# A graph attention product cut from 128 moving columns to the 32 of its head

## The reference

```python
h = (x @ W).reshape(n, heads, head_dim)            # 2048 x 4 x 32
src = jnp.einsum('nhd,d->nh', h, a[:head_dim, 0])
dst = jnp.einsum('nhd,d->nh', h, a[head_dim:, 0])
e = src[:, :, None] + dst.T[None, :, :]
e = jnp.where(e > 0, e, ALPHA * e)
e = jnp.where(mask, e, NEG_INF)
attn = jax.nn.softmax(e, axis=-1)
out = jnp.einsum('nhm,mhd->nhd', attn, h)           # the graph product
```

## Time and profile before

| what | value |
|---|---|
| median of 3 runs | 3480.16 us (3479.34 to 3480.24) |
| the profiled execution | 3477.87 us |
| its span, first to last instruction | 3476.2 us |
| PE busy | 2180.2 us (63%), 13842 records |
| PEld busy | 1526.6 us (44%) |
| DVE busy | 1950.8 us (56%) |
| ACT busy | 1052.5 us (30%) |
| POOL busy | 2078.4 us (60%) |
| mean granted TensorE clock | 0.774 of 2.4 GHz |

### The profile page before, as it was taken

The page is one execution under the profiler, slowest core; times in us unless marked ns, Lnnn a source line. Parts: engine busy times, 40 slices in busy tenths (PEclk is TensorE's granted clock), DMA queues, the critical chain, the costliest instruction groups (busy, mean ns, idle before and its releaser), DMA issues.

```text
span 3476.2 us, 42178 instructions
## 1 busy us (share of the span) xinstructions
PE 2180.2 (63%) x13842; PEld 1526.6 (44%) x13842; DVE 1950.8 (56%) x6499; ACT 1052.5 (30%) x1958; POOL 2078.4 (60%) x2078
## 2 busy tenths in 40 slices
PE   4425445555656565666666676868685767674776
PEld 4323333334334343444444454645463444454555
DVE  3577756565565656565757574747574521216543
ACT  2222222232222322333333333424242323232332
POOL 0026557777777777767777776767676777750000
PEclk7666666676777777777878787979797879887888
DMA  1013233434343334343434343333333344432110
GB/s 55 14 38 90 85 96 106 125 107 124 109 121 106 122 108 121 108 123 106 128 103 131 99 123 106 112 115 106 107 104 110 112 122 120 119 93 92 67 55 19
DMA packets 164634, 348.20 MB, mean 100 GB/s; under 512 B 38816, under 2 KB 91712, under 8 KB 160192
## 3 DMA queue, kind: packets, MB, share of 16 engines
q0 software_dynamic: 98624, 269.62, 26.4%
q1 hardware_dynamic: 65792, 75.90, 6.7%
HBM read 333.83 MB, written 11.53 MB: 99 GB/s over the span
## 4 chain that ended last, share of the span: by engine, by line
POOL 38%; PE 23%; issue 15%; DVE 14%; ACT 6%; DVEq 2%; DMA 2%; SPq 0%; ACTq 0%; POOLq 0%
POOL ring L571 38%; PE acc L652 9%; PE turn L643 5%; DMA ring<-in_kv_table,idxT 2%; PE wide L662 2%; PE rowsum L624 1%; DVE kv L1035 1%; ACT att_p L875 1%; PE turn L334 1%; PE wide L325 1%; DVE kv L1024 1%; ACT pt_sb L806 1%; DVE pos L1091 1%; DVE sims L1083 1%; ACT att_p L886 1%
## 5 line engine op out<-in xcount | busy, mean ns | idle before, releaser
L571 POOL DMA_INDIRECT ring<-in_kv_table,idxT x2048 | 2067.8, 1010 | 1028.7 <-issue 614.2
L624 PE MATMUL rowsum<-ring,w_block 128*32 128x256 f32 x4096 | 371.4, 464 | 512.7 <-DMA ring<-in_kv_table,idxT 487.7
L652 PE MATMUL acc<-kv,pt_sb 128*128 128x128 f32 x3968 | 623.5, 313 | 84.6 <-ACT pt_sb L806 84.5
L652 PEld LDWEIGHTS acc<-kv,pt_sb 128*128 128x128 f32 x3968 | 566.6, 222 | 130.8 <-ACT pt_sb L806 130.8
L806 ACT ACTIVATE pt_sb<-turn 128x512 f32<-128x512 f32 (+2 forms) x608 | 331.6, 562 | 474.1 <-PE turn L643 472.8
L624 PEld LDWEIGHTS rowsum<-ring,w_block 128*32 128x32 f32 x4096 | 103.6, 121 | 742.3 <-DMA ring<-in_kv_table,idxT 560.6
L643 PE MATMUL turn<-ident,kv 128*128 128x128 f32 x1280 | 253.1, 349 | 183.7 <-ACT kv L877 101.8
L643 PEld LDWEIGHTS turn<-ident,kv 128*128 128x128 f32 x1280 | 203.7, 184 | 233.5 <-issue 179.6
L730 PE MATMUL wide<-kv,qT 128*128 128x512 f32 (+3 forms) x576 | 261.0, 587 | 29.1 <-ACT att_p L886 20.7
L1048 DVE TENSOR_REDUCE att_m<-wide 128x1 f32<-128x128 f32 (+14 forms) x120 | 146.6, 1222 | 145.1 <-PE wide L730 140.4
L290 POOL DMA_DIRECT2D out<-ring x4 | 3.1, 773 | 362.5 <-DVE ring L453 362.5
(11 more groups left out here) (220 smaller groups left out, 3189.9 us busy)
## 6 DMA issues: line engine op xcount, KB each, us to landing
kv<-in_adj SPq DMA_DIRECT2D x32, 1024.0 KB, 5.0
ring<-in_kv_table,idxT POOLq DMA_INDIRECT x2048
wq_pair<-in_Wq SPq DMA_DIRECT2D x64, 128.0 KB
v_dram<-sums_sb SPq DMA_DIRECT2D x128, 64.0 KB
kv<-v_dram SPq DMA_DIRECT2D x16, 512.0 KB
att_p<-in_Wo SPq DMA_DIRECT2D x16, 512.0 KB, 4.7
xt<-in_x SPq DMA_DIRECT2D x16, 64.0 KB, 3.9
x_dram<-x SPq DMA_DIRECT2D x16, 64.0 KB, 2.2
```

Source lines behind the costliest of these rows:

```text
L571: pool.indirect_dma_start(ring[:, slot, i, :], None, kv_table, bass.IndirectOffsetOnAxis(idxT[:, r % 3, u:u + 1], 0))\
L624: mm = pe.matmul(rowsum[32 * k:32 * k + 32, 0:ROW], w_block[:, at:at + 32], ring[:, slot, k, :], start=(tk == 0), stop=(tk == 3))
L652: mm = pe.matmul(dst, pt_sb[:, q % 2, b * P:(b + 1) * P], rhs(4 * q + b), start=(q + b == 0), stop=(q == len(widths) - 1 and b == widths[q ...
```

## The change

In the call of `turn_and_sum` for the graph product, the moving operand becomes the 32 columns of head s instead of all 128 columns of h, and the result goes to the 32 columns of `acc` that line 1043 reads. Stationary operand, number of instructions, waits and buffers stay.

```diff
@@ -749,7 +749,8 @@
                     pe.wait_ge(gat_exp, m + 1)
                     after(pe, gat_out, m)
                     turn_and_sum(masked_dst, [4] * CH, gat_turned, gat_copied, m * CH,
-                                 lambda b: h_all[:, b * P:(b + 1) * P], acc[:, 2 * P:3 * P]).then_inc(gat_summed, 1)
+                                 lambda b: h_all[:, b * P + s * GD:b * P + (s + 1) * GD],
+                                 acc[:, 2 * P + s * GD:2 * P + (s + 1) * GD]).then_inc(gat_summed, 1)
                 if main:
                     pe.wait_ge(p_made, met(q, 2 * s) + 1)
                     scores_of(2 * s + 1)
```

## The result

The changed kernel takes 3587.24 us (median of 4 runs, 3584.24 to 3589.10) against 3480.20 us before (4 runs). The ratio is 1.0307, with a 95% interval of 1.0289 to 1.0325: 107 us slower. The number of instructions is the same, 42178.

What follows compares the result with a forecast made beforehand. No engine bounds the whole; POOL sets the pace from some 500 us to 3100 us. 78.4 + 2.6 + 10 - 1.4 = 89.6 us more on 3477.9 gave a forecast of 3568 us, range 3474 to 3600.

Steps and rivals of the forecast that it cites:

- part 1: Graph products on PE: a record costs the same at 8, 32 and 128 columns, so 0.00 us change for each.
- The small term of part 1: End of each graph product: the last record leaves the array sooner, 0.05 us each, 28 x 0.05 = 1.4 us gained.
- part 2: Graph products on PE: the clock doesn't rise within a changed product, 2.8 us lost for each, 28 x 2.8 = 78.4 us.
- (a): Graph products: clock rises as before and pace is as before, about 3479 us; chance 0.20.
- (b): Graph products: the clock rises in some products or later in them, 3490 to 3525 us; chance 0.10.
- First rounds: First four rounds: all 16 graph products on the path lose 2.8 us each, and line 704 loses 2.6 us in all.
- Step 3 of the later rounds: Rounds n = 1 to 12: the 12 graph products of step 3 have no cover and lose 2.8 us each.
- Rival (c): Graph products: narrow records run quicker than their weight loads suggest, 0.067 us each, 50 us gained, 3428 us; chance 0.12.
- the one for the late rounds: Last four graph rounds: PE's cover shrinks, 2.5 us lost on each, 10 us in all, bounds 0 and 34.

Runs made afterwards that it cites:

- the third experiment: Only the 12 graph products of step 3 in rounds n = 1 to 12 take 32 columns, against the kernel before: 3510.24 us, ratio 1.0085.
- The kernel with fillers: Changed kernel (32 columns) plus unread 512-column products in PE's idle time ahead of graph products, n = 9 to 12 excepted: 3518.96 us; 128 columns with the same: 3484.31.

## Why the prediction was right

It gave 3568 us, with 3474 to 3600 as the range and 0.68 for slower; the result is 3587.

The pace (part 1) holds. Start to start, the records of the graph products have a median of 0.213 us at 0.50 and 0.112 at 1.00, the same with 32, 64, 96 and 128 columns. (The prediction's 0.116 is an average over 16 records, one of which took 0.170 us; 3.27 us for 16 narrow ones at 0.50 is 0.204 each because their second record starts 0.074 us after the first.) What stays the same in all of them is the load of 128 stationary columns, and PEld is busy for 5.33 of PE's 5.65 us in the narrow product at 1.00; no run here changes that load alone, so that it sets the pace is the reading that fits and not one that was tested.

By the Trainium skill's bare gap rule (page "TensorE: Matmul & The Clock Gate", section "Back-to-back issue gap"), moving columns over the clock, an estimate for a record is a quarter of its time. The prediction left out the floor in the table of that section, some 60 cycles for 1 to 64 columns against 134 for 128, by which the estimate would have been a bit under half. Neither shows in the pace of any run here.

The small term of part 1 came out in size and not in cause. The prediction put it at 0 to 0.09 us and gave the last record's earlier end as its reason. At 1.00 the last record is followed by the next line after 111 ns at either width; the 0.08 us of the last group (1.76 against 1.85) lies at its start, in the 31 ns for 112. That the size fits is luck.

The clock (part 2) did what line 596 had suggested, and rivals (a) and (b) fell: one product in 64 saw a rise. The length forecast for such a product was 10.5 us and is 10.3; the loss for each on the path was 2.8 and is 2.6 by the chain of n = 5. Line 704 takes 1.89 us instead of 1.03, as forecast, and the steps of the first round are 20.9 us apart (the turns begin at 53.80 and 74.74). First rounds: forecast 47.4 us, measured 41.1 to 42. Step 3 of the later rounds: forecast 33.6, measured 31 in the third experiment, where only nine of the 12 stayed at 0.50. So this term was close, but the 31 is no test of 12 such products.

One step of part 2 goes too far: that the clock rises on account of the turns and products alone, since PE does nothing else in those stretches. Ahead of the product at the end of the round of n = 5 PE came from row sums without a gap. And the products of step 3 in the rounds n = 1, 3 and 7 saw the rise in the third experiment and did not see it in the changed kernel, at the same width of their own. The kernels differ in the products before them, but it is one trace each, and no run separates the work before a product from the chance of how the stretches fall.

Rival (c) fell with the pace. Its 0.067 us was no pace of records that follow each other: those of line 624 go to four strips of `rowsum` and start in bunches, most of them 7 ns behind the one before. The kernel with fillers shows what the change gains once the clock is no matter: 0.18 us for a product.

**The term that was mis-sized** is the one for the late rounds. The prediction put 2.5 us on each of the last four graph rounds, 10 us in all, with 34 as the upper bound. The experiment with narrow products in steps 0 to 2 alone lost 29 us, of which 22 in and behind these four rounds. The row that I had read (PE's wait for gathers down to 17.9 us in the round of n = 12) said that cover was left; what it doesn't say is where in the round it lies. The trace of the kernel before does, for the stretch of that round ahead of the first graph product's turns (at 2502.6 us) and for the one behind:

```profile
PE rowsum L624 <- DMA ring<-in_kv_table,idxT: 15.6, 6, 4.3
...
PE rowsum L624 <- DMA ring<-in_kv_table,idxT: 2.3, 3, 1.0
```

Three products that take 2.6 us more each can draw on 2.3 us and not on 17.9. With narrow products in steps 0 to 2 the same round still has 15.7 us of such waits, all ahead of the first product, and the turns of its steps begin 35.9 us apart on average instead of 32.4. In the round of n = 5 the part behind the first product's end was 24.3 of the 40.8 us, which covers them. It was wrong to add up the waits of a round as if a delay in any of its steps could draw on them.

The sum was 89.6 us and 107 came: 19 more in this term, 7 less in the others, and 5 that separate the whole from its three parts, within what their intervals allow. The two errors partly cancel, which is why the total looks better than the late rounds did.

What stays open: how the clock is decided in a mix of turns and products of one width and another. The runs show that it rose with 96 columns as with 128, in 24 products with 64 of the 59 that began low, and in hardly any with 32, in this mix and at this pace, and no more than that. Narrow products of one place rose in one kernel and not in another, so their width alone does not settle it.

## What to carry to other kernels

Cutting the moving operand of an f32 product that loads 128 stationary columns each time saved next to nothing here (0.18 us of 6.06 at the same clock): compare records with few and many moving columns start to start before counting on it. It cost 3%, by the clock: look at the granted clock over each stretch on the path, and ask what work it was that raised it there. A tensor engine that idles ahead of such a stretch can be given wide products to do, provided that they end before the stretch begins; here that was worth 1%, and the same with too many of them nothing. Before counting waits as cover, look at which side of the delayed work they lie on.

## What the runs showed of the hardware that I had not expected

- An engine kept busy for 7.00 us by records of 8 moving columns stayed at the lower clock, as did all 27 narrow fillers that began there; all 26 of 512 columns that began there reached the higher (with half the number of records it was 11 of 24). I had held the first for likely from one place in the trace; that it is so plain was new.
- The width of a product alone does not settle its clock: three narrow products at the end of their rounds saw the rise in the kernel where those before them were wide (6.5 to 6.7 us) and not in the one where those were narrow (10.3 us). Why is open.
- The dependence on width is steep: no loss at 96 columns (ratio 0.9995), 92 of 107 us at 64.
- A record of 512 moving columns in f32 takes about 0.43 us at 1.00 and 0.85 at 0.50 (the starts of the fillers' weight loads stand 0.43 and 0.85 us apart), which is how a filler becomes too long at the very clock that it is there to raise.
